# A vision tower on one NeuronCore: the last stage's norm as two VectorE steps a tile, two expert folds moved into the second stage's drain

## The reference, cut to what matters

```python
h = einsum('ecd,edf->ecf', disp, w1) + b1
y = einsum('ecf,efd->ecd', h, w2) + b2
out = where(keep, gate_val * y[slot], 0)
y2 = (z - mean(z)) * rsqrt(var(z) + eps) * g2 + be2      # z = y1 + out
return h1 + y2                                           # h1: the residual stream
```

## Time and profile before

| | us |
|---|---|
| median of 3 runs | 1268.35 |
| range of the runs | 1265.66 to 1270.06 |
| profiled execution, its own time | 1266.32 |
| its span | 1264.4 |
| first transpose of stage two's x2 | 544.6 |
| stage three begins | 1059.4 |
| first and last sum of stage three (L1546) | 1080.12, 1251.90 |
| busy: PE 1134.3, DVE 1000.9, POOL 886.2, ACT 776.5 | 90%, 79%, 70%, 61% of the span |

### The profile page before, as it was taken

The page is one execution under the profiler, slowest core; times in us unless marked ns, Lnnn a source line. Parts: engine busy times, 40 slices in busy tenths (PEclk is TensorE's granted clock), DMA queues, the critical chain, the costliest instruction groups (busy, mean ns, idle before and its releaser), DMA issues. The chain is left out here.

```text
span 1264.4 us, 36668 instructions
## 1 busy us (share of the span) xinstructions
PE 1134.3 (90%) x10938; PEld 1030.8 (82%) x10939; DVE 1000.9 (79%) x2811; ACT 776.5 (61%) x1714; POOL 886.2 (70%) x1193
## 2 busy tenths in 40 slices
PE   1999999999999999879988889898989874999994
PEld 1999999999999999778888888888888863666662
DVE  5588888888888888727977777777777767799997
ACT  3465555666566666447766666666666651678875
POOL 1566767666666677216888888888888884478887
PEclk9999999999999999989999999999999977999997
DMA  7435545454554553212333333333333325788882
GB/s 216 174 129 159 165 154 175 149 184 149 169 169 146 174 159 118 100 34 86 111 110 100 104 106 107 104 108 104 101 111 104 106 87 178 214 232 237 243 235 90
DMA packets 97312, 180.22 MB, mean 143 GB/s; under 512 B 12319, under 2 KB 62753, under 8 KB 96226
## 3 DMA queue, kind: packets, MB, share of 16 engines
q1 hardware_dynamic: 82500, 138.66, 36.4%
q0 software_dynamic: 13312, 39.75, 8.6%
q10 hardware_dynamic: 1440, 1.07, 0.3%
HBM read 112.69 MB, written 67.80 MB: 143 GB/s over the span
## 5 line engine op out<-in xcount | busy, mean ns | idle before, releaser
L528 POOL TENSOR_TENSOR xl<-xf,xh 128x512 fp32r<-128x512 f32 x141 | 184.9, 1339 | 167.8 <-ACT xh L447 167.8
L311 PE MATMUL ps_h<-wh,xh 128*128 128x256 f32 x588 | 165.7, 282 | 4.9 <-DVE xl L669 4.9
L311 PE MATMUL ps_h<-wh,xl 128*128 128x256 f32 x588 | 166.6, 283 | 0.0
L311 PE MATMUL ps_h<-wl,xh 128*128 128x256 f32 x588 | 166.5, 283 | 0.0
L1475 POOL DMA_INDIRECT out<-res,c_idx x106 | 124.1, 1171 | 43.0 <-issue 21.1
L1084 POOL DMA_INDIRECT bins<-rows,slot_i x98 | 101.7, 1038 | 59.1 <-POOL slot_i L1078 40.0
L1623 PE MATMUL c_ps_y<-w,yt 128*128 x424 | 118.2, 401 | 2.7 <-ACT c_py L1430 1.1
L311 PE MATMUL b<-x2h,wh 128*128 128x256 f32 x392 | 117.5, 300 | 2.6 <-DVE x2l L1102 1.8
L311 PEld LDWEIGHTS ps_h<-wh,xh 128*128 128x128 f32 x588 | 112.2, 191 | 5.7 <-DVE xl L669 5.7
L311 PE MATMUL b<-x2h,wl 128*128 128x256 f32 x392 | 113.5, 289 | 0.0
L311 PE MATMUL b<-x2l,wh 128*128 128x256 f32 x392 | 113.3, 289 | 0.0
(11 more groups left out here) (282 smaller groups left out, 4290.7 us busy)
## 6 DMA issues: line engine op xcount, KB each, us to landing
xf<-xt SPq DMA_DIRECT2D x49, 768.0 KB, 5.4
row<-bins SPq DMA_DIRECT2D x106, 257.5 KB
h_dram<-h1b SPq DMA_DIRECT2D x49, 256.0 KB, 5.5
x_dram<-x2o SPq DMA_DIRECT2D x49, 256.0 KB, 5.6
x<-x_dram SPq DMA_DIRECT2D x98, 128.0 KB, 2.7
rows<-h_dram SPq DMA_DIRECT2D x98, 128.0 KB
w1s<-w1t SPq DMA_DIRECT2D x8, 1024.0 KB, 6.8
w2s<-w SPq DMA_DIRECT2D x8, 516.0 KB, 5.9
```

What stands on the lines that cost most here:

```text
L311: last = nc.tensor.matmul(out_ps, a, b, start=(i == 0), stop=(i == len(terms) - 1))
L528: last = nc.gpsimd.tensor_tensor(xl[:, p, part], xf[:, p, part], xh[:, p, part].bitcast(F32), ALU.subtract)
```

## The change

- **Folds.** Experts 5 and 6 (`LATE`) are folded in stage two's drain: their weights are loaded into tiles of their own on SyncE's queue in steps 3 and 4 of stage two, and `late_fold` puts eight quarters between TensorE's last steps and behind the counting matmul, into the PSUM tile b_4. The counting matmul takes b_1. ScalarE copies the results. Stage one folds five experts in its steps and expert 7 in its drain; its loop ends at step 24, the rest is written out. The sums of the bias stay where they were.
- **Bias rows.** b12 gets 34 equal rows, b12s and `two_rows` 128: the high part stands in row 0, the low part in row 32, zeros (b12s) or unused ones elsewhere, and `two_rows` is 1 in rows 0 and 32. ScalarE makes the high part, VectorE the low one, in stage one. `split_bias` is gone.
- **Tables.** The table of the first 16 tiles (`FIRST`) is made on VectorE in stage two's drain, that of the others in stage three. SyncE waits for the first before its loads, for the second after the first eight pairs. One scan over 784 columns, with a factor that is 0 at each expert's first column, takes the place of eight. The thresholds are made in two slices. 12 matmuls that nobody reads take the place of 40.
- **Keep** is computed for two pairs at once.
- **Norm.** `centre` computes (z - mean)·g2 and `finish` its product with 1/dev plus the h1 row, each one VectorE instruction a tile of 128x256. ScalarE's norm and VectorE's gain and shift are gone. `scale` moves a step later, before `mean`.

```diff
+FIRST = 2 * DEPTH
...
+LATE = (5, 6)
+IDLE = 12
...
-        b12 = sb("b12", [2, NE, D])
-        b12s = sb("b12s", [2, NE, D], F32R)
-        two_rows = sb("two_rows", [2, P], F32R)
-        half = sb("half", [2, 2])
+        b12 = sb("b12", [RB, NE, D])
+        b12s = sb("b12s", [P, NE, D], F32R)
+        two_rows = sb("two_rows", [P, P], F32R)
...
+        def tables(v, link, lo, hi):
+
+            count, c = hi - lo, slice(lo, hi)
+            link(v.tensor_tensor(ge[:, c], tix[:, c].unsqueeze(2).to_broadcast([P, count, NE]),
+                                 nt[:, 2, :].unsqueeze(1).to_broadcast([P, count, NE]), ALU.is_ge))
+            v.tensor_tensor(gw[:, c], ge[:, c], nt[:, 3, :].unsqueeze(1).to_broadcast([P, count, NE]), ALU.mult)
+            link(v.tensor_reduce(tile_e[:, c], ge[:, c], AX_X, ALU.add))
+            link(v.tensor_reduce(tile_r[:, c], gw[:, c], AX_X, ALU.add))
+            link(v.scalar_tensor_tensor(tile_r[:, c], tix[:, c], float(P), tile_r[:, c], ALU.mult, ALU.add))
+            v.tensor_scalar(tab_e[:, c], tile_e[:, c], float(NE - 1), None, ALU.min)
+            return v.tensor_scalar(tab_r[:, c], tile_r[:, c], float(BINS), None, ALU.min)
...
-                run(sp, step, 0, NG + 6, 6, 42, FOLD)
+                run(sp, step, 0, NG + 6, 6, FOLD * (LATE[0] - 1), FOLD)
...
+                    if k.slot(FOLD) == 1 and k.back(2).valid(FOLD * NE):
+                        e = k.turn(FOLD) - 1
+                        wait(act, fb_out, e + 1)
+                        nc.scalar.activation(b12s[0:RB, bass.ds(e, 1), :].rearrange("p a d -> p (a d)"),
+                                             b12[:, bass.ds(e, 1), :].rearrange("p a d -> p (a d)"),
+                                             ACT.Copy).then_inc(fb_hi, 1)
...
+                def low_bias(k):
+                    if k.slot(FOLD) == 2 and k.back(3).valid(FOLD * NE):
+                        e = k.turn(FOLD) - 1
+                        wait(dve, fb_hi, e + 1)
+                        row, two = (a[LO:RB, bass.ds(e, 1), :].rearrange("p a d -> p (a d)") for a in (b12, b12s))
+                        v.tensor_tensor(two, row, two.bitcast(F32), ALU.subtract)
...
-                    if k.valid(FOLD * (NE - 1)):
+                    if k.valid(FOLD * LATE[0]):
...
+                    if isinstance(k.t, int) and k.c in (3, 4):
+                        for i in range(2):
+                            if k.c == 3:
+                                sp.dma_start(w1x[:, i, :], w1t[LATE[i]]).then_inc(wx_loaded, 16)
+                            else:
+                                sp.dma_start(w2x[:, i, :], w2[LATE[i], :, 0:FK * D]).then_inc(wx_loaded, 16)
...
+                def late_copy(i):
+                    act.wait_ge(late_ps, i + 1)
+                    A(w12[:, LATE[i], :], b_4[:], ACT.Copy).then_inc(late_out, 1)
+
                 run(act, step, 0, NG + 5, 6, 48, FOLD)
+                late_copy(0)
                 act.wait_ge(fi_ready, 1)
                 for e in range(NE // 2, NE):
                     r = act.value_load(fi[0:1, e:e + 1], min_val=0, max_val=BINS)
                     act.dma_start(bins[bass.ds(r, P), :], fill[:]).then_inc(filled, 16)
+                late_copy(1)
...
-                def split_bias(k):
-
-                    if k.valid(FOLD * NE):
-                        e, part = k.turn(FOLD), k.slot(FOLD)
...
-                    split_bias(k)
...
                 dve.wait_ge(Q["ohcopy"], NG)
-                v.memset(ones_j[:], 1.0).then_inc(row_ranks, 1)
+                link(v.tensor_scalar(cnt[:], cnt[:], float(P - 1), None, ALU.add))
+                link(v.tensor_copy(ci[:], cnt[:]))
+                link(v.tensor_scalar(nti[:], ci[:], 7, None, ALU.arith_shift_right))
+                link(v.tensor_copy(nt[:, 1, :], nti[:]))
+                v.tensor_tensor_scan(nt[:, 2, :], one8[:], nt[:, 1, :], 0.0, ALU.mult, ALU.add)
+                link(v.tensor_scalar(nt[:, 3, :], nt[:, 1, :], -float(P), float(BIN), ALU.mult, ALU.add))
+                tables(v, link, 0, FIRST).then_inc(tab_ready, 1)
                 v.tensor_copy(oht[:], oh_all[:].rearrange("p j e -> p e j")).then_inc(row_ranks, 1)
+                dve.wait_ge(row_ranks, 1)
+                v.tensor_tensor_scan(cinc[:].rearrange("p e j -> p (e j)"), restart[:].rearrange("p e j -> p (e j)"),
+                                     oht[:].rearrange("p e j -> p (e j)"), 0.0, ALU.mult, ALU.add).then_inc(row_ranks, 1)
                 dve.wait_ge(row_ranks, 2)
-                for e in range(NE):
-                    v.tensor_tensor_scan(cinc[:, e, :], ones_j[:], oht[:, e, :], 0.0, ALU.mult,
-                                         ALU.add).then_inc(row_ranks, 1)
-                dve.wait_ge(row_ranks, 2 + NE)
...
+                def late_fold(quarter):
+                    i, part, again = quarter // 4, quarter // 2 % 2, quarter % 2
+                    if quarter == 0:
+                        pe.wait_ge(wx_loaded, 4 * 16)
+                        pe.wait_ge(Q["k_out"], 2 * NG)
+                    if quarter == 4:
+                        pe.wait_ge(late_out, 1)
+                    for f in range(again * FK // 2, (again + 1) * FK // 2):
+                        last = mm(b_4[:, part * D:(part + 1) * D], w1x[:, i, f * D + part * P:f * D + (part + 1) * P],
+                                  w2x[:, i, f * D:(f + 1) * D], start=(f == 0), stop=(f == FK - 1))
+                    if quarter % 4 == 3:
+                        last.then_inc(late_ps, 1)
+
+                run(pe, step, 0, NG + 1, 6, 48, FOLD)
+                late_fold(0)
+                step(At(0, NG + 1, FOLD))
+                late_fold(1)
+                step(At(0, NG + 2, FOLD))
+                late_fold(2)
+                late_fold(3)
+                for c in range(NG + 3, NG + 4):
+                    step(At(0, c, FOLD))
+                late_fold(4)
                 pe.wait_ge(Q["acc"], 2 * NG)
-                pe.wait_ge(Q["k_out"], 2 * NG)
-                mm(b_4[:, 0:NE], ones_b[:], oh_acc[:], start=True, stop=True).then_inc(cnt_ps, 1)
+                pe.wait_ge(Q["et_out"], NG)
+                mm(b_1[:, 0:NE], ones_b[:], oh_acc[:], start=True, stop=True).then_inc(cnt_ps, 1)
+                for quarter in range(5, 8):
+                    late_fold(quarter)
...
-                run(sp, load, 0, PAIRS, *PAIR_LOOP, DEPTH)
+                for c in range(DEPTH):
+                    load(At(0, c, DEPTH))
+                sp.wait_ge(tab_ready, 2)
+                run(sp, load, DEPTH, PAIRS, *PAIR_LOOP, DEPTH)
...
-                def norm(k):
-                    p = k.slot(2)
-                    wait(act, nm_s, k.n() + 1)
-                    wait(act, zg_s, k.n() - 1)
-                    for i in range(2):
-                        nc.scalar.activation(zn[:, p, i, :], z[:, p, i, :], ACT.Identity, bias=nm[:, p, i:i + 1],
-                                             scale=rs[:, p, i:i + 1]).then_inc(zn_s, 1)
...
+                tables(v, link, FIRST, TILES).then_inc(tab_ready, 1)
...
                 def keep(k):
-                    b, p = k.slot(DEPTH), k.slot(2)
-                    wait(dve, loaded[b], (k.turn(DEPTH) + 1) * 32)
-                    wait(dve, py_s, k.n() * 2 - 2)
-                    v.tensor_tensor(below[:, p, :], row[:, b, :, OFF_S], tile_thr[:, bass.ds(k.n() * 2, 2)],
+                    if k.slot(2) == 1:
+                        return
+                    b = k.slot(DEPTH)
+                    n = 2 if k.back(-1).valid(PAIRS) else 1
+                    for i in range(n):
+                        wait(dve, loaded[b + i], (k.turn(DEPTH) + 1) * 32)
+                    wait(dve, py_s, k.n() * 2 - 4)
+                    v.tensor_tensor(below[:, 0:n], row[:, b:b + n, :, OFF_S],
+                                    tile_thr[:, bass.ds(k.n() * 2, n * 2)].rearrange("p (b i) -> p b i", b=n),
                                     ALU.is_lt).then_inc(below_s, 1)
-                    wait(dve, below_s, k.n() + 1)
-                    v.tensor_tensor(gk[:, p, :], below[:, p, :], row[:, b, :, OFF_GATE], ALU.mult).then_inc(gk_s, 1)
+                    wait(dve, below_s, k.turn(2) + 1)
+                    v.tensor_tensor(gk[:, k.slot(4):k.slot(4) + n], below[:, 0:n], row[:, b:b + n, :, OFF_GATE],
+                                    ALU.mult).then_inc(gk_s, 1)
...
                 def scale(k):
                     p = k.slot(2)
                     wait(dve, ve_s, k.n() + 1)
-                    wait(dve, zn_s, k.n() * 2 - 2)
                     v.reciprocal(rs[:, p, :], ve[:, p, :]).then_inc(rs_s, 1)
 
-                def shift(k):
+                def centre(k):
                     p = k.slot(2)
-                    wait(dve, rs_s, k.n() + 1)
-                    v.scalar_tensor_tensor(nm[:, p, :], mv[:, p, :, 0], -1.0, rs[:, p, :], ALU.mult,
-                                           ALU.mult).then_inc(nm_s, 1)
-
-                def gain(k):
```

(22 more changed lines are left out.)

151 lines of the change are left out of this document (69 added, 82 removed).

## The result

The kernel after takes 1280.85 us in the median of four runs (1277.11 to 1285.15), the kernel before 1268.48 beside it (1265.66 to 1270.06). The ratio is 1.010, with a 95% interval of 1.0073 to 1.0127: slower by 1%, where 27 us less were forecast. The profiled execution has a span of 1277.1 us, 12.7 over that of before.

The account below looks back on a forecast made before the run. Bounds taken: TensorE in stage one, GpSimd in stage two, VectorE and TensorE both full in stage three. +0.4 - 14.2 - 17 + 0.5 + 0 - 1.5 + 4.7 = -27.1, so 1268.35 - 27.1 gives 1241 us, range 1227 to 1259.

Parts of the forecast that it names:

- The setup: Before stage one: three more dependent small steps cost +0.4 us, the 128x2048 memset nothing.
- Stage one: Two of eight folds leave TensorE's full steps: 8 quarters x 1.77 us, -14.2 us.
- Stage two: Steady steps: GpSimd, taken as the pace, loses the bias splitting, -17 us; four weight loads on SyncE's queue cost +0.5.
- my end of -21: Stage two: the largest gain allowed for, if GpSimd alone sets the pace; the other end was 0.
- my bound of 5: Stage two: a stall from the four 1 MB weight loads was bounded by 0 and about 5 us.
- Drain and start of stage three: Drain taken as 0; then row loads not awaiting tables -1.3, slow first pairs +1, later reciprocal -1.2: together -1.5 us.
- TensorE's tile: Stage three: with 128 rows for the bias matmul a tile goes from 1.37 to some 0.98 us, hidden behind VectorE.
- The drain that the prediction names: Stage three, TensorE: a change of tiling mode drains the array, which would make the two-row matmul dear; no size given.
- A pair: Stage three, VectorE: a new pair of 3.30 us against 3.23 (40 pairs) and 3.13 (11), +4.7 us.
- The ends of my range: Stage three pair: 2.99 us (-11) with 0.33 a step and no wait; 3.45 (+12) with 0.40 and register work.
- a falling clock in stage three: Rival: TensorE's idle time lowers its clock, the pair takes 4.9 us at 1.2 GHz, 1283 us in all; chance 0.06.
- the order of TensorE: Rival: TensorE's order, not GpSimd, paces stage two, so -17 becomes 0 and the total 1258 us; chance 0.15.

Follow-up runs that it names:

- e6: The kernel before with the folds of experts 5 and 6 left out and nothing of the bias changed; 1282.0 us, one run.
- e8: The kernel before without GpSimd's split_bias; 1238.4 us, ratio 0.9751 to 0.9809.
- e1: The kernel after with 100 tiny unread matmuls in the setup, which move TensorE's later code; 1259.5 us.
- e10: e9 with the old norm and the 34-row bias load issued last; 1251.4 us, a total the study doesn't use.
- e16: The very kernel of e10 run once more; 1235.4 us, ratio 0.9742 to 0.9777.
- e3: The kernel after with the 34-row bias load issued later and VectorE's wait for it moved to step 5; 1264.3 us.
- e9: The kernel after with the fold part alone undone: no late folds, no weight loads in stage two; 1259.5 us.
- e15: The very kernel of e7 run once more; 1246.8 us, ratio 0.9833 to 0.9868.
- e7: e1 with the norm of the kernel before, the capacity test for two pairs kept; 1246.9 us.
- e12: The kernel before with 64 tiny matmuls (128 instructions) in the setup, moving stage two's loop; 1313.1 us, one run.
- e2: The kernel before with 35 tiny matmuls (70 instructions) in the setup, moving stage two's loop; 1278.4 us.

## Why the prediction was wrong, step by step

**The setup (+0.4, found +8.0).** I counted the three small steps and the memset, which cost nothing, and left out the DMA that the change widens from 16 to 272 KB at the head of SyncE's queue. My own list asked for each queue that a step is put ahead of.

**Stage one (-14.2, found -0.5).** This is the step that failed first in size. "8 quarters x 1.77" took the 8.93 us that a step without a fold had in the old trace for the pace of all such steps, and so took the room on VectorE as free: the forecast 14.2 us are only 3.2 (e6), as steps with two accumulations and no fold then take 9.9 to 10.2 us. The comparison in the earlier trace rows was a fair one, since its step without a fold has two accumulations too, as VectorE's timeline of before shows just behind that step's first transpose at 304.14:

```profile
304.22 1.00 DVE L658 SCALAR_TENSOR_TENSOR acc<-w2s,acc 128x256 f32<-128x256 f32 x2
```

VectorE's work fits into it, 8.0 of 8.95 us. What I had wrong is that this busy time stays as it is: behind GpSimd's subtraction it grows to 9.0 and more, and VectorE sets the pace. The earlier trace rows could not tell this, as their window of 440 to 505 us lies in the undisturbed rhythm.

**Stage two (-17 and +0.5, found -2.7).** The mechanism was right and too small: without the splitting it gives -29.8 (e8), beyond my end of -21. TensorE does 8.7 to 9.8 us a step and not 9.43 and up, and the half-clock stretches go too; that they go with GpSimd's pace is my reading. The weight loads cost 2 to 5 us by the excess of the steps behind them (3 in after), and 8 in e1, over my bound of 5. What ate the gain I had not thought of: three stops of 5 us with their slow restart, by the steps' excess over 9.2 us 22 us in all. -29.8 + 22 + 3 = -5, for the -2.7 found. More than that can't be told: e10 and e16, the same kernel, differ by 4.8 us in this stage.

**Drain and start of stage three (-1.5, found -1.5).** The row loads no longer wait for the tables, as forecast: SyncE's queue waits in after only for the fills there (3.8 us). The number is right, but the same stretch takes 64.0 to 66.1 us in e1, e3, e9, e15 and e16, so it proves nothing.

**TensorE's tile (1.37 to some 0.98, found 0.99).** The size is right, and its split is not. The bias matmul still takes 0.31 us start to start, not my 0.12. Instead the wait ahead of it is gone: behind the fourth pass it started after 0.31 us with two rows and starts after 0.03 with 128. The Trainium skill, TensorE: Matmul & The Clock Gate, section LDWEIGHTS (loading the stationary operand), says that a weight load's time goes with its columns and not with its rows. The trace agrees for the load itself, 0.18 us with two rows and 0.20 with 128. But it does not follow that the tile stays as long, as the prediction has it by that rule. What the two-row matmul cost is idle time before its weight load, 31.2 us at 94 of them before and 2.6 after. The drain that the prediction names would look so; no run tells it from another cause.

**A pair (+4.7, found +10.6).** Right sign, mis-sized. The new pair was put at 3.30 us and takes 3.48 on the average of its two kinds, 3.51 with the loop's turns. The scalar operand took 0.40 us, my upper end, for 0.37: 4 x 0.03 = 0.12 us. The wait before the aggregates came as forecast (0.93 from statistics to aggregates, 0.91 forecast). A second such wait I had missed: in every other pair no test stands between the sum and its statistics, 0.72 us instead of 0.61, 0.06 a pair. On the other side I took the old pair at 3.23 and 3.13, without the loop's turns, where its mean is 3.30; this put 0.09 too much into the forecast loss and so covered part of the error. The ends of my range don't follow from their terms either: 3.30 less 4 x 0.04 and the wait of 0.25 is 2.89 and not 2.99, unless the reciprocal takes the 0.10 between, and 3.30 with 0.12 and 0.1 for register work is 3.52 and not 3.45, and so near the 3.51 found. e1 against e7 prices the new norm: 12.6 us lost.

**The rivals.** The one on the slower side (a falling clock in stage three) was not the cause, though the clock did fall a little, and the order of TensorE was not the pace of stage two. None of mine was the true one: the load at the head of the queue, VectorE as the limit in steps without folds, and the place of the code.

## What to carry to other kernels

Taking work from the busiest engine is worth only what the second engine leaves, and the second engine's busy time in the old trace is not a constant: two engines that hold each other up can take up a slower rhythm once the pace changes. So leave the work out for a trial first, as e6 does, before you move it. After every change of a long loop's surroundings look at the instruction queue in the DMA view: packets within a loop whose instructions had stayed before point to its place and not its content, and moving the code by some instructions can give the time back (21 us in e1). And put a load that nobody needs yet behind those that are awaited.

## What the runs showed that I had not expected

TensorE keeps a loop of 1613 instructions if it touches seven packets of 256, and not for long if it touches eight: +44 us (e12), and +11 us where only what is fetched ahead can reach the eighth (e2). A VectorE instruction that meets GpSimd's subtraction is held for up to its length: a scan of 0.73 us took 1.71 to 1.83, a small instruction of 0.16 us took 1.24, and 0.07 us between the two starts decided it. A load that copies one row to 34 partitions delays what stands behind it by 6 to 8 us for 272 KB, while 1 MB of weights lands in 6.8 us by the page of before. And a matmul whose weights have two rows, between matmuls with 128, costs 0.3 to 0.4 us a tile more than one filled up to 128 rows with zeros.
